# Linear attention with an FFN: the attention output split in place and turned by four DMA transposes

## What is computed

```python
xn = _layernorm(x, axis=-1)
x = x + _L0_attn_ref(xn, ...) + _L0_ffn_ref(xn, ...)

# attention: h=64 heads, d=8
q = softmax(be * heads(xn @ Wq.T + bq)); k = softmax(be * heads(xn @ Wk.T + bk))
v = heads(xn @ Wv.T + bv)
kv = cumsum(einsum('zsD,zsd->zsDd', k, v), axis=1); kn = cumsum(k, axis=1)
out = einsum('zsD,zsDd->zsd', q, kv) / sum(q * kn, axis=-1)
return out @ Wo.T + bo

# FFN: x rounded to fp8 e4m3, einsum('bsi,oi->bso', x_dq, w_dq) + bias
```

## Time and profile before

| | us |
|---|---|
| median of 3 runs | 1250.56 |
| lowest and highest run | 1250.27, 1251.45 |
| the profiled execution, its own time | 1250.03 |
| its span, first to last instruction | 1248.2 |

### The profile page before, as it was taken

The page is one execution under the profiler, slowest core; times in us unless marked ns, Lnnn a source line. Parts: engine busy times, 40 slices in busy tenths (PEclk is TensorE's granted clock), DMA queues, the critical chain, the costliest instruction groups (busy, mean ns, idle before and its releaser), DMA issues.

```text
span 1248.2 us, 60447 instructions
## 1 busy us (share of the span) xinstructions
PE 1174.9 (94%) x26082; PEld 679.2 (54%) x26082; DVE 977.9 (78%) x1968; ACT 744.9 (60%) x1177; POOL 321.6 (26%) x590
## 2 busy tenths in 40 slices
PE   1459999999999999999999999999999999999996
PEld 1235555555555555555555555555555555555553
DVE  4567887888788788878878887788788778878873
ACT  0456656665666666566666656666665666566652
POOL 3122222322222232222223232222323232222310
PEclk9689999999999999999999999999999999999999
DMA  9022334334334433433333343343343433333331
GB/s 234 21 59 70 81 90 89 78 80 91 82 82 87 89 80 79 90 86 80 85 89 82 77 90 89 78 84 91 81 79 91 84 83 81 91 82 81 72 73 46
DMA packets 156483, 104.64 MB, mean 84 GB/s; under 512 B 111968, under 2 KB 128480, under 8 KB 156256
## 3 DMA queue, kind: packets, MB, share of 16 engines
q1 hardware_dynamic: 155536, 99.76, 35.7%
q10 hardware_dynamic: 720, 1.31, 0.4%
HBM read 40.20 MB, written 16.78 MB: 46 GB/s over the span
## 4 chain that ended last, share of the span: by engine, by line
PE 92%; issue 3%; DVE 2%; DMA 1%; ACT 1%; POOL 1%; SPq 0%; POOLq 0%; DVEq 0%; ACTq 0%
PE s_ps L900 10%; PE a_ps L917 7%; PE a_ps L1018 6%; PE a_ps L999 6%; PE k_ps L873 5%; PE vo_ps L975 5%; PE vo_ps L873 5%; PE k_ps L877 5%; PE k_ps L875 5%; PE vo_ps L884 4%; PE vo_ps L888 4%; PE vo_ps L886 4%; PE vo_ps L877 4%; PE vo_ps L875 4%; PE q_ps L877 4%; PE q_ps L873 4%
## 5 line engine op out<-in xcount | busy, mean ns | idle before, releaser
L521 ACT ACTIVATE q_heads<-qT,cst 128x512 f32<-128x512 f32 x256 | 163.9, 711 | 88.2 <-DVE qT L769 88.2
L407 POOL TENSOR_TENSOR y_sum<-y,y_magic 128x512 f32<-128x512 f32 x64 | 81.4, 1272 | 433.0 <-DVE y_magic L629 433.0
L506 ACT ACTIVATE w_own<-kT,cst 128x512 f32<-128x512 f32 x128 | 85.5, 715 | 166.7 <-DVE kT L711 166.7
L530 ACT ACTIVATE st_seqs<-st_run,cst 128x576 f32<-128x576 f32 x252 | 181.5, 797 | 0.5 <-DVE st_run L665 0.5
L671 DVE TENSOR_TENSOR att<-s_ps,cst 128x512 f32<-128x512 f32 x256 | 163.8, 682 | 0.4 <-PE s_ps L900 0.4
L400 POOL TENSOR_TENSOR x_split<-xn,x_split 128x512 f16<-128x512 f32 x64 | 74.1, 1158 | 291.6 <-ACT x_split L462 284.3
L900 PE MATMUL s_ps<-q_heads,w_own 64*64 64x128 f32 x4096 | 141.3, 275 | 0.6 <-DVE att L671 0.6
L900 PEld LDWEIGHTS s_ps<-q_heads,w_own 64*64 64x64 f32 x4096 | 110.4, 132 | 54.3 <-issue 54.2
L462 ACT ACTIVATE x_split<-xn 128x512 f16<-128x512 f32 x64 | 40.3, 630 | 126.7 <-DVE xn L618 126.7
L873 PE MATMUL k_ps<-w_hi,xT 128*128 128x512 f16 x256 | 98.9, 386 | 17.0 <-DMA xT<-x_split 12.3
L727 DVE TENSOR_TENSOR vp<-vo_ps,vp 128x512 f32<-128x512 f32 x64 | 44.3, 692 | 86.3 <-PE vo_ps L877 86.3
(11 more groups left out here) (136 smaller groups left out, 2287.8 us busy)
## 6 DMA issues: line engine op xcount, KB each, us to landing
v_groups<-vp SPq DMA_DIRECT2D x512, 36.0 KB, 3.1
x_in<-L_attn_x SPq DMA_DIRECT2D x64, 256.0 KB
x_res<-L_attn_x SPq DMA_DIRECT2D x64, 256.0 KB
out<-o_sb SPq DMA_DIRECT2D x64, 256.0 KB
w_own<-L_attn_Wk SPq DMA_DIRECT2D x1, 1024.0 KB, 13.0
w_own<-L_attn_Wq SPq DMA_DIRECT2D x1, 1024.0 KB, 15.0
w_own<-L_attn_Wv SPq DMA_DIRECT2D x1, 1024.0 KB, 16.5
att<-L_ffn_weight_fp SPq DMA_DIRECT2D x1, 1024.0 KB, 18.1
```

The source lines that it names most:

```text
L506: last = sc.activation(k_pairs[:, i.parity, :, c, :], kT[:, :, :], ACT.Copy, scale=pair_mask[:, c:c + 1])
L521: last = sc.activation(q_heads[:, i.parity, :, j, :], qT[:, i.parity, :, :], ACT.Copy, scale=head_mask[:, j:j + 1])
L530: last = sc.activation(st_seqs[:, i.parity, :, :, b, :].rearrange("p g j w -> p (g j) w"), st_run[:, :, :, :].rearrange("p g j w -> p (g j ...
```

## The change

The attention output is no longer turned by TensorE. ScalarE copies `a_n` to a f16 high part, GpSimd forms the low part, both in one tile `a_split` in SBUF, and SyncE turns that tile by four transposing DMAs, 32 partitions each, into `aT`. The output product then reads `aT`. The bank of `t_ps` becomes `o_ps`, for the FFN and output products; `vo_ps` holds V alone. On TensorE the V projection moves ahead of the FFN product, so that the inter and the intra product are neighbours. On VectorE the low part is gone, `scale_values` moves up behind `add_state`, and `output` is last. On SyncE `turn_a(i-2)` is the first of a body and `move_v(i)` comes behind the load of x.

```diff
@@ tiles
-        ah = sb("ah", [P, J, P], F16)
-        al = sb("al", [P, J, P], F16)
+        a_split = sb("a_split", [P, 2, SEQS, G * DH], F16)
+        aT = sb("aT", [P, J, 2, SEQS, TOK], F16)
@@ sync
+            def turn_a(t):
+                sp.wait_ge(al_ready, (t + 1).n)
+                if t.after(1):
+                    sp.wait_ge(o_done, t.n)
+                else:
+                    sp.wait_ge(bvo_done, 1)
+                for u in range(J):
+                    sp.dma_start_transpose(aT[:, u].rearrange("p h b s -> p (h b) s"),
+                                           a_split[TOK * u:TOK * (u + 1)].rearrange("p h b r -> p (h b r)"))\
+                        .then_inc(a_turned, 16)
             def body(i):
-                if (i - 1).exists():
-                    move_v(i - 1)
+                if (i - 2).exists():
+                    turn_a(i - 2)
                 if (i + 1).exists():
                     turn_x(i + 1)
                 if i.exists():
                     turn_xq(i)
                 if (i + SLOTS).exists():
                     load_x(i + SLOTS)
+                if i.exists():
+                    move_v(i)
@@ gpsimd
+            def low_attention(t):
+                pool.wait_ge(ah_ready, (t + 1).n)
+                if t.after(1):
+                    pool.wait_ge(a_turned, t.n * 16 * J)
+                gp.tensor_tensor(flat(a_split[:, 1]), a_n[:, :, :, :].rearrange("p b g d -> p (b g d)"),
+                                 flat(a_split[:, 0]), ALU.subtract).then_inc(al_ready, 1)
             def body(i):
+                if (i - 2).exists():
+                    low_attention(i - 2)
@@ scalar
-                    sc.activation(vo_ps[:, :], bias[:, 3, :], ACT.Copy, scale=out_up[:, :])\
+                    sc.activation(o_ps[:, :], bias[:, 3, :], ACT.Copy, scale=out_up[:, :])\
                         .then_inc(oseed_ready, 1)
+                    act.wait_ge(an_ready, (t + 1).n)
+                    if t.after(1):
+                        act.wait_ge(a_turned, t.n * 16 * J)
+                    sc.activation(flat(a_split[:, 0]), a_n[:, :, :, :].rearrange("p b g d -> p (b g d)"), ACT.Copy)\
+                        .then_inc(ah_ready, 1)
-                    act.wait_ge(aT_done, (t + 1).n)
-                    if t.after(1):
-                        act.wait_ge(o_done, t.n)
-                    sc.activation(flat(ah[:, :, :]), t_ps[:, :], ACT.Copy).then_inc(ah_ready, 1)
@@ vector
-                if (i - 2).exists():
-                    dve.wait_ge(ah_ready, (i - 1).n)
-                    v.tensor_tensor(flat(al[:, :, :]), t_ps[:, :], flat(ah[:, :, :]), ALU.subtract)\
-                        .then_inc(al_ready, 1)
-                if (i - 2).exists():
-                    output(i - 2)
                 if t.exists() and i.exists():
                     add_state(t)
+                if i.exists():
+                    scale_values(i)
                 if (i + 3).exists():
                     statistics(i + 3)
                 if i.parity == 0 and (i + PAIR).exists():
                     variances(i + PAIR)
-                if i.exists():
-                    scale_values(i)
+                if (i - 2).exists():
+                    output(i - 2)
@@ tensor
-                    for b in range(SEQS):
-                        last = transpose(t_ps[:, :].rearrange("p (j b s) -> p b j s", b=SEQS, s=TOK)[:, b],
-                                         a_n[:, b, :, :].rearrange("p g d -> p (g d)"), ident)
-                    last.then_inc(aT_done, 1)
+                if i.exists():
+                    if i.after(1):
+                        pe.wait_ge(vp_ready, i.n)
+                    project(vo_ps, i, MV, seeded=False).then_inc(v_done, 1)
@@ tensor, behind the FFN product
-                    pe.wait_ge(ah_ready, (t + 1).n)
-                    pe.wait_ge(al_ready, (t + 1).n)
+                    pe.wait_ge(a_turned, (t + 1).n * 16 * J)
                     project_out(rest=True).then_inc(o_done, 1)
@@ tensor, between the inter and the intra product
-                if i.exists():
-                    if fold:
-                        pe.wait_ge(fold_ready, 1)
-                    if (i - 2).exists():
-                        pe.wait_ge(o_ready, (i - 1).n)
-                    project(vo_ps, i, MV, seeded=False).then_inc(v_done, 1)
```

## The result

| | before | changed |
|---|---|---|
| median of 4 runs each, us | 1250.99 | 1393.51 |
| lowest and highest | 1250.27, 1251.45 | 1388.27, 1409.32 |
| span of the profiled execution | 1248.2 | 1389.7 |
| from the start of body 2 to that of body 64 | 1124.32 | 1242.29 |

In the changed kernel, and in the kernel with the whole pair on GpSimd in experiment 4, one of the four executions was over 1.5% longer than the fastest (here 1409.32); ratios and differences leave it out, and the median of the other three here is 1391.54. The ratio is 1.113 (95% interval 1.109 to 1.116): slower, as forecast, but by 141 us where 19 were predicted, and far outside the range. The 62 bodies take 20.04 us each in place of 18.13, +118 us. The tail from body 64 on is 1389.7 - 1345.74 = 44.0 us in place of 23.4, +20.6. Body 2 starts 3.0 later.

The account below looks back on a forecast made before the run. TensorE's products bound the kernel. Span 1248.2 + 2 (62 bodies, transposes saved but a new wait for the turns) + 17 (last two bodies) = 1267.2, plus 1.83 around it: 1269 us, range 1224 to 1300.

Parts of the forecast that it names:

- TensorE alone needs 17.55 us a body, and the output product could start at place 12.43: TensorE's body: 18.04 less 0.49 us of transposes; output product at 10.22 - 0.49 + 2.70 from the first K product.
- V's moves start at 13.47 and `x_res` is issued at T = 20.2: SyncE: moves start about 13.47 after the first K product; 6.11 us of moves and 0.65 of store put x_res at 20.2.
- The turns wait for the pair in the DMA queues: Attention-output turns queue behind store and x_res load, which fill four DMA engines; ready 11.0 us after x_res issue, at 31.2.
- c: Time from issue of x_res to the turns being ready: 11.0 us, bounds 10.0 and 12.
- The prediction's own formula: Output product's wait: a late body follows an early one, so twice the mean wait is 31.2 - 29.98 = 1.22 us.
- P = 17.55 + w: Steady body: TensorE's 17.55 us plus a mean wait of 0.61 for the turns, 18.16 us; +2 us over 62 bodies.
- SyncE's load 16.3 us: SyncE's issues in a body: 11.05 us plus four turns of 1.3 each, 16.3, under the 18.16 us body.
- SyncE becomes the bound: Rival: turns take over 1.78 us to issue, or SyncE's queue stalls; 1290 or about 1376 us; chance 0.17.
- Its other form: SyncE stands until store and x_res load have drained: 19.9 us a body, +109, about 1376 us; within the 0.17 chance.
- The first rival: Turns do not wait behind store and x_res load: 17.55 us a body, 1228 us, or 1222 with seam savings; chance 0.15.
- The tail, +17: Last two bodies: output product waits +8.3 and +6.1 us for the turns, low clock costs 1.3 us twice.
- The start, nothing: Bodies 0 and 1: no change in time, since the products there stay the same.

Follow-up runs that it names:

- experiment 4: Changed kernel, store and x_res load in pieces: on ScalarE 1354.94 us, in ScalarE's waits 1261.51, on GpSimd 1261.28; both whole on GpSimd 1602.66.
- Experiment 1: Changed kernel with store and x_res load issued ahead of V's moves on SyncE: 1278.15 us; issued by ScalarE at its body's start: 1343.63 us.
- experiment 2: x_res loads beyond the first two left out: in the changed kernel 1260.53 us; in that with the store ahead of V's moves 1243.04 us.
- experiment 3: Kernel before plus four idle transposes a body: behind store and x_res load 1584.54 us, ahead of x_in load 1261.16; plain copies behind x_res load 1271.27.
- the kernel that halves the dose and puts the pair ahead: Changed kernel with the store issued ahead of V's moves and x_res loads beyond the first two left out: 1243.04 us.
- The last run: Kernel of 1259.41 us (store and all loads in pieces on GpSimd), with the last two steps' attention output turned on TensorE: 1249.26 us.

## Why the prediction was right or wrong

*TensorE alone needs 17.55 us a body, and the output product could start at place 12.43.* Right: 17.58, and 717.16 - 3.45 - 701.22 = 12.49.

*V's moves start at 13.47 and `x_res` is issued at T = 20.2.* Nearly. In the undisturbed body they start at 737.68 - 723.66 = 14.0; where SyncE was late, at 15.7. T was 744.48 - 723.66 = 20.8 and 722.84 - 701.22 = 21.6, with a median of 21.0.

*The turns wait for the pair in the DMA queues and are ready at T + 11.0, bounds 10 to 12.* The mechanism is right (experiments 1, 2 and 4), the size is not: 12.5. I had taken four transposes behind the pair for little more than one plain move behind it. With T about 1 us and c 1.5 us larger, the wait was 68.7 / 62 = 1.1 us a body on average, not 0.61: +31 us. The prediction's own formula would make (21.0 + 12.5 - 29.98) / 2 = 1.8 of it; the `issue` waits and the low clock also lengthen bodies and leave the turns more time, but how much of the gap that is no run isolates.

*P = 17.55 + w: a body is TensorE's own time and the wait for the turns.* This is the step that failed: the price of turns that stand behind the pair. The waiting of the output product was in the sum, too small by 31 us. Two further terms were put at nothing. I charged the clock in the last two bodies and nowhere else, though the steady bodies were to hold the same wait; there it was up to 34 us, 20 of them behind waits for the turns. And the 46 us of `issue` waits were nowhere in the sum nor in a rival; experiment 3 shows such waits alone, up to 6.2 us each, with no reader of the turns. About 30 of the 46 us go with the pair. 31 + 34 + 46 = 111 of the 116 us by which 62 bodies of 20.04 exceed 62 of 18.16; the other 5 are the 0.1 us by which 17.55 was short.

*SyncE's load 16.3 us.* Low: turns of 1.55 each (6.18 / 4) and a turn of x at 2.58 in the body shown. The pair is not the reason for that: with every long DMA in pieces (1259 us) four turns still took 5.6 us and a turn of x 2.15 in the median. But SyncE is not the bound; it waited 108 us for `a_split` and 46 us for `vp`. The rival "SyncE becomes the bound" gave 19.9 us a body and 1376 us, close to the 20.04 measured. Experiment 1 refutes its plain form: relief of 1.2 us a body gained less than a mere reordering did. Its other form, a queue that takes no more until the pair has drained, is seen in the 10.84 us of experiment 3. In the changed kernel it shows in 3 of 64 bodies, where the turns took 9.8 to 10.7 us to issue, body 64 among them; the median is 5.7. That the number came close was luck.

*The first rival, turns that do not wait for the pair, 1228 us.* Out; but the kernel that halves the dose and puts the pair ahead, at 1243 us, comes near to what it described.

*The tail, +17.* Measured +20.6. In body 64 the output product started 1360.35 - 1345.74 = 14.6 into the body, +9.9 where +8.3 were forecast. In body 65 it started 1377.43 - 1367.85 = 9.6 behind the end of the intra product, +6.0 where +6.1 were forecast. The low clock cost 2.3 us twice and not 1.3: each of the two output products took 5.0 us in place of 2.7. The last run confirms the cause for most of it: from the start of body 64 to the end it takes 28.8 us, against 42.3 in the kernel it was made from and 23.4 before.

*The start, nothing.* It was +3.0 in this execution; over the other kernels with the change body 2 starts anywhere from 98.9 to 103.6 us, so this says nothing of the change.

## What to carry to other kernels

Before adding a DMA transpose, list every DMA in flight around it by the number of engines it uses: one with a leading dimension of 4 should be cut into pieces along it or be issued so early that it has drained. Ahead is not safe either if the long DMA starts within a microsecond. A wait on TensorE costs its length and, when the clock falls, more: here 3.45 us cost 4.8, while 3.28 us cost 3.28. Price the clock from the mean over the whole stretch, not from one body. Test a doubtful DMA as an idle one in the kernel before, in the place where the change would put it: one run would have shown that place to be ruinous.

## What the runs showed of the hardware

- Four transposes of 32 rows by 1024 f16 columns a body cost 11 us over 64 bodies with the DMA engines drained, and 334 us right behind 512 KB of 4 x 32 x 512 transfers. Plain copies of as many bytes in that bad place cost 20 us.
- While transposes are stuck, engines that wait for none of them stand as well: TensorE up to 6.2 us, and SyncE's issues took 10.84 us for four. 45 of 200 instruction packets took over 4 us there (longest 8.3), none over 1.7 us with plain copies.
- The clock fell behind 13 of 31 waits of TensorE for the turns; a wait of 2.48 us was among them, one of 3.28 us was not.
- A DMA of 4 x 32 x 512 f32 and four of 32 x 512 move the same bytes; from GpSimd the whole pair took 1.42 us to issue, the eight pieces 3.97, and the kernels took 1602.66 and 1261.28 us.
- Eight DMA issues on ScalarE held its next instruction for 6.88 us; put into its waits they cost nothing that could be seen against GpSimd's.
